# A decoder megakernel: projections dealt anew between the stages, a shorter quantisation, and no idle products in the last pass

## What is computed

```python
x = ln(x + attention_16_heads_of_64(x))            # attn0
x = ln(x + cross_attention_16_heads_of_16(x, ctx)) # cross0
x = ln(x + bitlinear_ffn(x))                       # ffn0
x = ln(x + gated_decay_attention_and_mlp(x))       # attn1
x = ln(x + cross_attention_softmax_over_queries(x, ctx)) # cross1
x = ln(x + three_coupled_cycles(x))                # coupled_ffn
```

## Time and profile before

| | |
|---|---|
| median of 3 runs | 1112.31 us (1110.94 to 1112.71) |
| the profiled execution | 1113.01 us |
| its span, first to last instruction | 1111.2 us |
| granted TensorE clock, mean | 0.996 of full speed |
| steady pass (second, third) | 265.0 us |

### The profile page before, as it was taken

How to read it: one execution, slowest core, us unless ns; L and a number is a source line. 1 busy time by engine, 2 the same in 40 slices (tenths; PEclk the granted TensorE clock), 3 DMA queues, 4 the chain that set the end, 5 groups by cost and what they waited for, 6 DMA issues and landing times.

```text
span 1111.2 us, 19750 instructions
## 1 busy us (share of the span) xinstructions
PE 1033.7 (93%) x7232; PEld 683.8 (62%) x7232; DVE 797.5 (72%) x1880; ACT 636.4 (57%) x1728; POOL 311.6 (28%) x666
## 2 busy tenths in 40 slices
PE   9999999998989999999899999999899988898886
PEld 5577457855566655775657745775556765576463
DVE  3684886668697588648788588666869758864777
ACT  2582656386586357459478355647648724644833
POOL 1264102341065301142117420224105630224110
PEclk9999999999999999999999999999999999999999
DMA  9350000000010000000000000000000000000000
GB/s 339 85 158 1 20 10 1 1 1 1 1 40 2 20 1 9 1 1 1 1 20 21 1 20 1 10 1 1 1 1 20 2 1 1 1 1 1 1 1 20
DMA packets 16432, 22.78 MB, mean 20 GB/s; under 512 B 2257, under 2 KB 14033, under 8 KB 16209
## 3 DMA queue, kind: packets, MB, share of 16 engines
q1 hardware_dynamic: 15472, 20.85, 5.7%
q10 hardware_dynamic: 864, 0.68, 0.2%
HBM read 19.42 MB, written 2.10 MB: 19 GB/s over the span
## 4 chain that ended last, share of the span: by engine, by line
PE 54%; DVE 28%; ACT 10%; issue 6%; POOL 3%; DVEq 0%; POOLq 0%; ACTq 0%
PE PS L534 8%; PE PS L952 5%; PE PS L717 4%; ACT work L1425 3%; PE PS L703 3%; PE PS L666 3%; PE PS L921 3%; DVE stat L1791 2%; PE PS L565 2%; PE PS L966 2%; PE PS L683 2%; PE PS L812 2%; POOL rstd L2390 2%; DVE maxx L1997 2%; PE PS L509 2%
## 5 line engine op out<-in xcount | busy, mean ns | idle before, releaser
L2390 POOL TENSOR_TENSOR rstd<-var,minus_half 128x2 f32<-128x2 f32 x64 | 45.9, 717 | 523.5 <-DVE var L1804 523.5
L1651 ACT ACTIVATE work<-PS,nmax 120x256 f32<-120x256 f32 x256 | 118.3, 486 | 18.3 <-DVE nmax L2228 17.7
L2228 DVE TENSOR_REDUCE nmax<-PS 120x2 f32<-120x512 f32 x128 | 82.3, 685 | 35.3 <-PE PS L952 35.1
L1425 ACT ACTIVATE work<-PS,nmax 128x256 f32<-128x256 f32 x176 | 81.6, 487 | 17.6 <-DVE nmax L1864 17.6
L1864 DVE TENSOR_REDUCE nmax<-PS 128x2 f32<-128x512 f32 x128 | 82.2, 677 | 10.6 <-PE PS L666 10.6
L2404 POOL TENSOR_SCALAR work<-work,inv 128x256 f32<-128x256 f32 x176 | 81.7, 486 | 0.0
L2385 POOL TENSOR_TENSOR pool_pause<-minus_half 128x1 f32<-128x1 f32 x96 | 28.8, 300 | 179.8 <-DVE inv L1871 91.6
L666 PE MATMUL PS<-work 64*128 64x256 f32 x512 | 70.0, 397 | 5.9 <-ACT work L1425 5.6
L1378 ACT COPY turned_a<-PS 128x512 f32<-128x512 f32 x24 | 14.2, 590 | 100.9 <-PE PS L509 100.9
L666 PEld LDWEIGHTS PS<-work 64*128 64x128 f32 x512 | 44.6, 186 | 24.2 <-ACT work L1425 14.2
L717 PE MATMUL PS<-wo,work 128*128 128x256 f32 x256 | 58.5, 384 | 0.0
(11 more groups left out here) (278 smaller groups left out, 2557.0 us busy)
## 6 DMA issues: line engine op xcount, KB each, us to landing
xa<-in_x_dram SPq DMA_DIRECT2D x4, 512.0 KB, 4.0
out_dram<-x_room SPq DMA_DIRECT2D x7, 256.0 KB, 2.2
rows<-in_rows_dram SPq DMA_DIRECT2D x1, 1536.0 KB, 10.8
turned_x<-in_x_turned_dram SPq DMA_DIRECT2D x3, 512.0 KB, 3.5
late<-in_L_attn_W_dram SPq DMA_DIRECT2D x2, 768.0 KB, 8.2
wq<-in_attn_q_dram SPq DMA_DIRECT2D x1, 1024.0 KB, 9.2
wk<-in_attn_k_dram SPq DMA_DIRECT2D x1, 1024.0 KB, 11.2
late<-in_ffn_gate_dram SPq DMA_DIRECT2D x1, 1024.0 KB, 13.1
```

Source lines behind the costliest of these rows:

```text
L1425: op = act.activation(e0[u % 3][:, st, hh, :], bank(2 * (u % 2) + hh)[:, st * S:(st + 1) * S], ACT.Exp, bias=nmax0[:, u % 2, hh, st:st + 1 ...
L1651: op = act.activation(e1[:, par, r, kv, :], bank(SCORE_1[r])[0:M, kv * S:(kv + 1) * S], ACT.Exp, bias=nmax1[:, par, r, kv:kv + 1], accum_o ...
L2228: dve.tensor_reduce(nmax1[:, par, r, :], bank(SCORE_1[r])[0:M, :].rearrange("p (v s) -> p v s", v=2), AX.X, ALU.max, negate=True).then_inc ...
```

## The change

1. Full passes (0 to 2): the halves and quarters of the next pass's projections stand in other places, on TensorE and in ScalarE's copies. Their number is the same.
2. Quantisation: `amax` is clipped and divided by 127 in one instruction, and its reciprocal is the scale. The instruction that multiplied the inverse by 127 is gone: two for each pass in `quantize`, four in the loop over t, 24 in all. The signals of these steps are renamed to fit. VectorE's write of `xq` waits for `turn_x` of unit 6 in addition.
3. The last pass has its own order of cross0 and ffn0 on TensorE, ScalarE and VectorE, and all 45 idle products are left out.
4. The table of ScalarE's functions loaded at the end of ffn0 is one that holds both the exponential and the logarithm, so that one table load for each pass (line 1595) is gone.

TensorE's two helpers first, of which the second goes, and then its order in the last third of coupled_ffn:

```diff
             def values0(it, n, halves=(0, 1)):
...
-            def spin(n, to=7):
-
-                for _ in range(n):
-                    pe.matmul(bank(to)[:, 0:S], ones[:, :], upto[:, :], start=True, stop=True)
...
-                if then is not None:
-                    keys0(then, 6, (2,))
-                else:
-                    spin(1)
                 net_4(it, 2, 0)
                 if then is not None:
-                    keys0(then, 6, (3,))
                     pe.wait_ge(z_crossed_done.sem, z_crossed_done.at(it, NB))
                     scores0(then, 0)
-                else:
-                    spin(4)
+                    keys0(then, 6, (2, 3))
                 net_2(it, 2, 1)
+                if then is not None:
+                    keys0(then, 7, (0,))
                 turn_final(it, 0, then)
```

TensorE's cross0 of the last pass:

```diff
+            def cross0_last(it):
...
+                scores_x(it, 4)
+                turn_x(it, 2)
+                weigh_x(it, 0)
+                turn_x(it, 3)
                 scores_x(it, 5)
                 scores_x(it, 6)
                 turn_x(it, 4)
                 weigh_x(it, 1)
+                turn_x(it, 5)
                 scores_x(it, 7)
                 turn_x(it, 6)
+                out_x(it, 0)
                 weigh_x(it, 2)
                 turn_x(it, 7)
                 weigh_x(it, 3)
                 out_x(it, 1)
+                turn_quantized(it, 0)
```

TensorE's cross1, full passes:

```diff
                     scores_1(it, n)
                     if n == 0:
                         turn_normed(it, "x4", xs["4"], 1)
-                    if then is not None and n == 2:
-                        queries0(then, 7)
+                    if then is not None and n in (0, 4):
+                        queries0(then, 7, (n // 4,))
...
+                    if then is not None and n in (12, 20):
+                        keys0_whole(then, 0, (n - 12) // 8)
                     if n == 20:
                         turn_back(it, 0)
-                    if then is not None and n in (12, 16, 20):
-                        keys0_whole(then, (n - 12) // 8, 1 - n // 4 % 2)
+                    if then is not None and n == 24:
+                        keys0_whole(then, 1, 0)
                     if n == 24:
                         turn_normed(it, "z0", aff, 0)
...
+                    if then is not None and n == 30:
+                        keys0_whole(then, 1, 1)
                     if n % HP == 2 and n > HP:
                         weigh_1(it, n // HP - 1)
-                if then is None:
-                    spin(1)
-                else:
-                    keys0_whole(then, 1, 1)
                 weigh_1(it, 2 * GX - 1)
```

ScalarE's table, VectorE's `quantize`, and VectorE's new order for the last pass:

```diff
-                load_table(ACT.Exp)
+                act.preload_act_table_set("natural_log_exp_and_others")
...
-                    dve.tensor_scalar(amax[:, h], amax[:, h], 1e-5, None, ALU.max).then_inc(a_clip.sem, 1)
-                    dve.wait_ge(a_clip.sem, a_clip.at(it, hf + 1))
-                    dve.reciprocal(qinv[:, h], amax[:, h]).then_inc(a_inv.sem, 1)
-                    dve.tensor_scalar(gate_scale[:, h], amax[:, h], w_mean[:, 0:1], 1.0 / 127, ALU.mult, ALU.mult)
...
-                    dve.wait_ge(a_inv.sem, a_inv.at(it, hf + 1))
-                    dve.tensor_scalar(qscale[:, h], qinv[:, h], 127.0, None, ALU.mult).then_inc(a_scale.sem, 1)
+                    dve.tensor_scalar(amax[:, h], amax[:, h], 1e-5, 1.0 / 127, ALU.max, ALU.mult).then_inc(a_step.sem, 1)
+                    dve.wait_ge(a_step.sem, a_step.at(it, hf + 1))
+                    dve.reciprocal(qscale[:, h], amax[:, h]).then_inc(a_scale.sem, 1)
...
+                if it == NI - 1:
...
+                    subtract_x(7)
+                    sum_2(0)
+                    divide_x(2)
+                    apply_norm(it, "2", of(res), xs["2"], 0)
+                    divide_x(3)
+                    quantize(0)
+                    sum_2(1)
+                    apply_norm(it, "2", of(res), xs["2"], 1)
+                    product(0)
+                    quantize(1)
+                    scale_product(0)
```

More of the change, by code:

```diff
@@ L1190, in cross0 @@
                 turn_x(it, 2)
-                weigh_x(it, 0, then)
+                weigh_x(it, 0)
+                turn_x(it, 3)
                 scores_x(it, 5)
-                turn_x(it, 3)
-                if then is not None:
-                    values0(then, 2)
                 scores_x(it, 6)
@@ L1231, in ffn0, with ffn0_last @@
                 up(it, 1)
[L1232 to L1235 removed]
+                values0(then, 7)
+                gate(it, 2)
+                up(it, 2)
+                queries0(then, 0, (0,))
+                turn_hidden(it, 0)
+                gate(it, 3)
+                context1(it, 1)
+                queries0(then, 0, (1,))
+                up(it, 3)
+                turn_hidden(it, 1)
+                down(it, 0)
+                queries0(then, 1)
+                turn_hidden(it, 2)
+                down(it, 1)
+                queries0(then, 2)
+                turn_hidden(it, 3)
+                down(it, 2)
+                queries0(then, 3, (0,))
+                down(it, 3)
+            def ffn0_last(it):
+                gate(it, 0)
+                up(it, 0)
+                context1(it, 0)
+                gate(it, 1)
+                up(it, 1)
+                turn_quantized(it, 1)
+                context1(it, 1)
                 gate(it, 2)
@@ L1655, in cross1 @@
                         keep_q0(then, 7)
-                    if then is not None and n == 18:
+                    if then is not None and n == 19:
                         keep_k0(then, 0)
@@ L1768, in one_pass @@
                 attn0(it, last)
-                cross0(it, then)
-                ffn0(it, then)
+                cross0_ffn0(it, then)
                 if first_pass(it):
```

411 lines of the change are left out of this document (230 added, 181 removed).

## The result

The changed kernel takes 1115.55 us (median of 12 runs, 1114.51 to 1119.46), the kernel before 1112.7 us beside it: a ratio of 1.0034, 95% interval 1.0022 to 1.0045. It is slower by a third of a per cent, where 1105.2 us and "faster" was forecast, and it lies outside the range of 1098.5 to 1112.4 us. The profiled execution is the fastest of the twelve: 1114.51 us, with a span of 1112.8 us and a mean granted clock of 0.979 instead of 0.996. Each trace is of one execution, so what it says of the last pass is one draw of several.

The account below looks back on a forecast made before the run. Neither TensorE nor VectorE bounds it alone; the chain alternates between them. Full passes 6.8 plus last pass 3.3 less clock 3.0 gives 7.1 us off the profiled 1113.0, with the median 0.7 lower: 1105.2 us, range 1098.5 to 1112.4.

Parts of the forecast that it names:

- (i): Last pass without idle products: two more clock falls on the chain, 3.0 us lost.
- (f): Last pass: all six shortened quantisation steps count, 1.1 us gained.
- R1: Rival: in the last pass every long wait lets the clock fall, ten more falls, 1117 us; chance 0.08.
- (b): Full passes, cross1: half key projections moved, one into the gap before turning z0; 1.0 us a pass, bounds 0 and 1.23.
- (c): Full passes: last query projection cut in two around a pair of scores; 0.2 us a pass, bounds 0 and 0.45.
- (e): Full passes: all other moves (query 3 and 5, keys 4 to 7, ScalarE's copies) worth nothing; bounds -0.5 and +1.0 us.
- R2: Rival: gaps are VectorE's own, its chain keeps its length in cross1, moved projections gain nothing; 1109.5 us, chance 0.22.
- (g): Last pass, new order of cross0: first output projection and second sum come sooner; 1.7 us, bounds 0 and 2.2.
- (a): Full passes, cross0: half the second value projection moves behind the first turning, into gaps; 0.86 us a pass.
- (d): Full passes: shorter quantisation, mostly covered by TensorE's own work in ffn0; 0.2 us a pass.
- (h): Last pass: one group of idle products on the chain goes; 0.5 us gained, ends 0 and 2.16.

Follow-up runs that it names:

- new_no_five: Changed kernel with all idle products put back (first set and eight more) except five behind cross1's first output projection: 1105.06 us.
- new_old_cross1: Changed kernel with the old places of query 7 and keys 0 to 3 in full passes: period 264.19 us, one run 1117.51 us.
- old_last_order: Kernel before with the shorter quantisation and eight more idle products at long waits, old order of cross0 and ffn0 kept: 1109.01 us.
- old_quant: Kernel before with the shorter quantisation alone, six VectorE instructions fewer a pass: period 264.75 us, one run 1110.4 us.
- old_half_value: Kernel before with one half of the second value projection behind cross0's first turning in full passes: period 264.08 us, single run 1111.94 us.
- new_more_idle: Changed kernel with 51 idle products put into the last pass, eight of them at waits left unfilled before: 1105.52 us, ratio 0.9936.
- new_best: new_more_idle with the old places of keys 4 to 7 in full passes: 1104.08 us, ratio 0.9929.

## Why the prediction was wrong

The step that failed most is (i): "I take two more falls on the chain, 3.0 us". Measured by the same order with and without idle products (new_no_five, which has all but the five on the chain), the clock costs the changed kernel 207.79 - 197.92 = 9.87 us. The kernel before already paid 203.13 - 200.90 - 0.8 = 1.43 of it (0.8 is what (f) measured), all at z0. So it is 8.4 us more, not 3.0. R1 had the mechanism and its own rule is met (a mean clock under 0.93 behind 903 us: 0.89), with a price of 15 us in all that was too high and a chance of 0.08 that was too low. Nor is "what a fall costs" known, as (i) says: the fall from which it took its 1.5 us, that of 929 us in cross0, cost the kernel before nothing, the one at z0 cost 1.5 us, and the same fall behind turning 7 costs 1.7.

The Trainium skill's page "TensorE: Matmul & The Clock Gate", section "HAM oscillation — how this bites in real kernels", tells of a clock that falls back to half in the waits between bursts of products, again and again; its case waits for DMA, and longer. The traces agree in kind: 14 windows of 4 us under 0.9 against two, behind waits for ScalarE and VectorE of 1 to 3.1 us. The forecast set that aside with two waits that had brought no fall, those of 1.37 and 1.23 us. Both lie between dense work, the first right behind a group of idle products, the second in a full pass; neither shows what such a wait does when its neighbours are empty too. The counter-argument in R1, that only 24 of 174 busy us were idle products, counted their sum where their places decide.

The second step that failed is (b), with (c) and (e). This is R2, and it came together with the clock, where the forecast had held them as alternatives. The sum with the measured sizes: 1105.2 + 5.4 for (i) + 3.7 for the full passes (6.8 - 3.06) - 0.5 for (f) and (g) = 1113.8 us. That is the profiled execution's 1114.51 less the 0.7 by which I had put the median below the profile. It must come out so, since the sizes are differences of the same landmarks; it checks no mechanism. The median came out 1.0 above the profiled execution, and its mean clock does not say why: it is 0.979 at 1114.51 us, 0.977 at 1115.52 and 0.978 at 1119.39.

Point by point:

- (a) right: 0.86 forecast, 0.94 a pass measured alone.
- (b) and (c) wrong: 1.2 us a pass forecast, -0.05 measured, within what the period varies. This is R2. The wait of 1.23 us before the turning of z0 went, as forecast; the half projection filled it, and left the pass no shorter, because a wait of 0.74 us for ScalarE opened where that half had stood. The argument against R2, that VectorE had waited for a pair of scores behind a half projection, is what failed: without the half the pair waits for ScalarE. "Near the upper end" had no row behind it but the size of the gap. So the chain that keeps its length there runs through ScalarE's exponentials as well as VectorE; which of its steps holds it was not tested by itself.
- (d) right in the steady period, 0.27 for 0.2; over all passes 1.8 us for 0.6.
- (e) wrong: not nothing, but a loss of 0.4 us a pass for keys 4 to 7. The bound of -0.5 held.
- Together (a), (d), the 0.16 us that cross0 of the last pass comes later in new_old_cross1, and (e) would give 2.72 + 1.80 + 0.16 - 1.04 = 3.64 us up to cross0 of the last pass; 3.06 were measured. The remaining 0.6 us, moves in ffn0 and attn1 or parts that overlap, were not taken apart; the 0.16 us are within the 0.35 by which the five kernels with the changed full passes differ there (905.01 to 905.36 us).
- (f) a little high: 1.1 forecast, 0.8 measured. From the landmark, ffn0's first sum starts after 963.92 - 908.07 = 55.85 us in the kernel before and 55.07 us in old_last_order; it now waits 0.28 us for TensorE, which is where the rest went.
- (g) right in cross0, 1.7 forecast and 1.93 measured, within its bound of 2.2; the 0.5 us that the order of ffn0 adds had no term. Together 2.46.
- (h) right: 0.5 and 0.5.
- The lower end of the range says that it takes (a) to (e) at their upper bounds, but puts 0.8 for (e), whose bound is 1.0. With that the end would be 1097.8 us; it changes nothing here.

With (f), (g) and (h) at their measured sizes, 0.8 + 2.46 + 0.5 us, and the clock of the kernel before, the last pass would have gained 3.8 us; the clock took 8.4. So the gain of the new order is real, and was paid back more than twice over by the idle products that went with it.

## What to carry to other kernels

Products that compute nothing are not priced by where they stand on the chain: take them out and read the granted clock, window by window, of everything behind them. When waits sit close together, fill all of them: here one filled of two did not keep the fall away. What a fall costs depends on where it lies: inside a wait that TensorE would have had anyway it was free, at the output projection one turning later it cost 1.7 us. And a gap on a busy engine that a moved piece of work fills is no gain unless the engine it waited for also comes sooner: test by moving that piece alone, and read the period.

## What the runs showed of the chip

A wait alone does not decide whether the clock falls. TensorE's timeline at the turning of z0 in the last pass, the kernel before and then the changed one:

```profile
1046.67 0.66 PE L509 MATMUL PS<-ident,x_room 128*128 128x128 f32 x4 [1.75 <-DVE x_room L2188]
1047.35 1.88 PE L952 MATMUL PS<-x_room,work 64*120 64x256 f32 x8
```

```profile
1043.38 0.66 PE L506 MATMUL PS<-ident,x_room 128*128 128x128 f32 x4 [1.74 <-DVE x_room L2272]
1044.06 1.13 PE L949 MATMUL PS<-x_room,work 64*120 64x256 f32 x8
```

The instructions and the waits are alike, 1.75 and 1.74 us; behind the one the scores take 1.88 us (a clock of 0.57 in the earlier trace rows), behind the other 1.13 us (1.00 in the window of 1044 to 1048 us). The two differ by where the program stands, 3.3 us apart, and by what ran before. The waits of 1.57 and 1.83 us in cross0 say the same: in old_quant and old_half_value TensorE runs the same products around them, and the output projection behind took 1.99 us in one and 3.68 in the other. The spread shows it too: the twelve runs of the changed kernel have mean clocks of 0.977 to 0.983 and times of 1114.51 to 1119.46 us, while kernels whose waits are filled repeat within 0.3 us (new_more_idle), 0.7 us (new_best) and 0.9 us (old_last_order), and only new_no_five has one execution over 1.5 us above its others. What decides between two such waits stays open.
